# Where the late row blocks of W are staged, and in which order the transfers behind them are issued

## What is computed

```python
xc     = einsum('bct,bcd->bdt', x, w_cond[idx])             # 32 batches of 128 x 2048
result = einsum('bnd,od->bno', xc, W_base) + b_base          # 2048 x 2048 weights
logits = einsum('bnd,ed->bne', xc, W_gate)                   # 8 experts
route  = softmax(logits), top 2, renormalised
h      = einsum('bnd,erd->bner', xc, A)                      # rank 16
delta  = einsum('bner,eor->bno', h * route, B)
out    = x + result + delta
```

## Time and profile before

| | us |
|---|---|
| median of 3 runs | 1579.82 (1578.82 to 1580.52) |
| the profiled execution's own time | 1577.55 |
| its span, first to last instruction | 1575.7 |
| TensorE busy in the span | 1507.3 (96%) |
| VectorE busy | 1350.8 (86%) |
| ScalarE, GpSimd busy | 619.0 (39%), 645.7 (41%) |

### The profile page before, as it was taken

The page is one execution under the profiler, slowest core; times in us unless marked ns, Lnnn a source line. Parts: engine busy times, 40 slices in busy tenths (PEclk is TensorE's granted clock), DMA queues, the critical chain, the costliest instruction groups (busy, mean ns, idle before and its releaser), DMA issues.

```text
span 1575.7 us, 25846 instructions
## 1 busy us (share of the span) xinstructions
PE 1507.3 (96%) x9427; PEld 809.4 (51%) x9427; DVE 1350.8 (86%) x2258; ACT 619.0 (39%) x1016; POOL 645.7 (41%) x516
## 2 busy tenths in 40 slices
PE   5779999999999999999989999999999999999998
PEld 4554554555445554555545455555455555455553
DVE  6897999999899999999868888888888788888875
ACT  6665444444543445444413332223332223332321
POOL 3664555665666555665532122122122122122122
PEclk9899999999999999999999999999999999999999
DMA  5345555655555555655797343344343344333342
GB/s 192 108 158 166 163 163 166 191 169 167 152 165 171 166 160 178 179 185 155 220 344 246 105 127 101 95 141 130 113 124 93 105 141 124 118 116 93 114 111 74
DMA packets 169567, 235.95 MB, mean 150 GB/s; under 512 B 71898, under 2 KB 88794, under 8 KB 167130
## 3 DMA queue, kind: packets, MB, share of 16 engines
q1 hardware_dynamic: 167426, 219.63, 46.2%
q10 hardware_dynamic: 2016, 14.68, 2.4%
HBM read 147.83 MB, written 86.43 MB: 149 GB/s over the span
## 4 chain that ended last, share of the span: by engine, by line
PE 72%; DVE 15%; issue 5%; DMA 3%; POOL 2%; ACT 2%; SPq 0%; DVEq 0%; ACTq 0%; POOLq 0%
PE bank_x L1450 8%; PE bank_x L1451 8%; PE bank_x L1452 8%; PE bank_y L1452 8%; PE bank_y L1451 8%; PE bank_y L1450 8%; PE bank_z L1451 2%; PE bank_z L1452 2%; PE bank_z L1450 2%; DVE t_sums L1086 2%; PE bank_h L1452 2%; PE bank_h L1450 2%; PE bank_h L1451 2%; PE bank_c L1450 2%; PE bank_c L1452 2%
## 5 line engine op out<-in xcount | busy, mean ns | idle before, releaser
L608 POOL TENSOR_TENSOR x_res<-x_res,t_sums 128x512 f32<-128x512 f32 x255 | 350.2, 1376 | 847.6 <-DVE t_sums L1091 688.9
L1450 PE MATMUL bank_x<-TT,s_parts 128*128 128x512 f16 x768 | 294.4, 383 | 7.2 <-DVE s_parts L1061 5.9
L1451 PE MATMUL bank_x<-TT,s_parts 128*128 128x512 f16 x768 | 293.8, 383 | 0.0
L1452 PE MATMUL bank_x<-TT,s_parts 128*128 128x512 f16 x768 | 293.4, 382 | 0.0
L1450 PE MATMUL bank_y<-TT,s_parts 128*128 128x512 f16 x768 | 291.1, 379 | 2.3 <-DVE TT L1201 2.3
L1451 PE MATMUL bank_y<-TT,s_parts 128*128 128x512 f16 x768 | 291.1, 379 | 0.0
L1452 PE MATMUL bank_y<-TT,s_parts 128*128 128x512 f16 x768 | 291.1, 379 | 0.0
L716 ACT ACTIVATE p_copies<-bank_x,y_inv 128x512 f32<-128x512 f32 x128 | 87.7, 685 | 416.1 <-PE bank_x L1452 317.0
L1091 DVE TENSOR_TENSOR t_sums<-t_sums,inv_w 128x512 f32<-128x512 f32 x255 | 232.3, 911 | 8.7
L1061 DVE TENSOR_TENSOR s_parts<-a_full,s_parts 128x512 f16<-128x512 f32 x224 | 191.2, 870 | 33.7 <-ACT s_parts L701 33.7
L580 POOL TENSOR_TENSOR x_res<-x_res,BT 128x512 f32<-128x512 f32 x128 | 206.7, 1615 | 24.1 <-DMA x_res<-in_x_dram 22.8
(11 more groups left out here) (242 smaller groups left out, 2751.7 us busy)
## 6 DMA issues: line engine op xcount, KB each, us to landing
x<-in_x_dram SPq DMA_DIRECT2D x32, 1024.0 KB, 6.0
x_res<-in_x_dram SPq DMA_DIRECT2D x128, 256.0 KB, 4.0
part_scratch<-x_res SPq DMA_DIRECT2D x128, 256.0 KB, 3.0
x_res<-part_scratch SPq DMA_DIRECT2D x128, 256.0 KB, 4.0
out_dram<-x_res SPq DMA_DIRECT2D x128, 256.0 KB, 3.1
wt_scratch<-late_words SPq DMA_DIRECT2D x64, 224.0 KB, 3.5
TT<-wt_scratch ACTq DMA_DIRECT2D x14, 1024.0 KB, 9.2
x_parts<-in_L_ffn_W_base_dram SPq DMA_DIRECT2D x18, 512.0 KB, 6.6
```

The source lines that it names most:

```text
L608: nc.gpsimd.tensor_tensor(XR[:, xr_slot(m), :], XR[:, xr_slot(m), :], TM[:, m % 2, :], ALU.add).then_inc(r_added, 1)
L1450: nc.tensor.matmul(dst, lhs[0], rhs[0], start=start, stop=False, skip_group_check=chained)
L1451: nc.tensor.matmul(dst, lhs[0], rhs[1], start=False, stop=False, skip_group_check=chained)
L1452: return nc.tensor.matmul(dst, lhs[1], rhs[0], start=False, stop=stop, skip_group_check=chained)
```

## The change

Unit 5 is staged in the bias's place, unit 6 in x's place and unit 7 in A's place. The bias and step 1's x are loaded behind them. SyncE's order, ScalarE's, VectorE's, GpSimd's and TensorE's are rewritten to match; `w_scales` and the arithmetic are as before.

```diff
         def rows_of(g, i):
             if g < NU // 2:
                 return early_rows[(2 * g + i) % 4]
-            return (X, af_rows, xp_rows, af_rows)[g - NU // 2][:, i, :]
+            if g == NU // 2 + 1:
+                return bias[:, i * KH:(i + 1) * KH]
+            return (X, None, X, af_rows)[g - NU // 2][:, i, :]
...
@@ SyncE
             sp.wait_ge(w_tr, 4 * (NU // 2))
-            sp.dma_start(bias, b_base...).then_inc(bias_in, 16)
+            load_rows(5)
             for m in range(2, 4):
                 load_tile(m)
             sp.wait_ge(s_lo, NPROD)
-            load_rows(5)
-            sp.wait_ge(f_lo, 2)
-            sp.dma_start(ft_dram, FT_second...).then_inc(ft_out, 16)
+            load_rows(7)
             sp.wait_ge(b_lo, 1)
             sp.dma_start(bt_dram, BT_first).then_inc(bt_out, 16)
             sp.wait_ge(w_tr, 4 * 5)
+            load_rows(6)
+            sp.wait_ge(f_lo, 2)
+            sp.dma_start(ft_dram, FT_second...).then_inc(ft_out, 16)
+            sp.wait_ge(w_tr, 4 * 6)
+            sp.dma_start(bias, b_base...).then_inc(bias_in, 16)
+            sp.wait_ge(w_tr, 4 * 7)
             load_x(1)
-            sp.wait_ge(ft_out, 16)
-            load_rows(6)
             store_tile(0)
-            sp.wait_ge(w_tr, 4 * 6)
-            load_rows(7)
@@ GpSimd
+            w_lower(4)
+            w_lower(5)
             pool.wait_ge(bias_in, 16)
             add_bias(0)
+            add_r(0)
             add_bias(1)
-            w_lower(4)
-            add_r(0)
+            add_r(1)
+            w_lower(6)
             add_bias(2)
-            w_lower(5)
-            add_r(1)
             add_bias(3)
-            w_lower(6)
             add_r(2)
             add_r(3)
             w_lower(7)
@@ ScalarE
             nc.scalar.copy(inv_b[:, :], BD[:, 0:ER]).then_inc(agb_inv, 1)
+            sum_rows(5)
             copy_p(0, 0, P1_COPY)
             w_upper_first(4)
             copy_p(0, 0, P5_COPY)
-            sum_rows(5)
-            w_upper_rest(4)
+            upper(4, 2, B22)
+            upper(4, 3, B21)
+            sum_rows(6)
+            w_upper_sums(4, (T1, T3, T2, T4))
             copy_p(0, 0, U2_COPY)
             copy_p(0, 0, P4_COPY)
             w_upper_first(5)
-            sum_rows(6)
+            sum_rows(7)
             w_upper_rest(5)
-            sum_rows(7)
             w_upper(6)
             w_upper(7)
+            act.wait_ge(ft_out, 16)
             split_x_hi(1, 0)
@@ VectorE
             finish(0, 0, C11)
             w_first_sum(5)
-            find_maxima(1)
             w_scales(6)
             w_other_sums(5)
             finish(0, 0, C12)
             w_first_sum(6)
             w_scales(7)
             w_other_sums(6)
-            find_top(1)
             finish(0, 0, C21)
             finish(0, 0, C22)
             w_first_sum(7)
+            find_maxima(1)
+            w_other_sums(7)
+            find_top(1)
             scale_x(1)
-            w_other_sums(7)
             split_x_lo(1, 0)
@@ TensorE
             w_quad(6, 2)
             w_quad(6, 3)
+            w_quads(7)
             transpose_maxima(1)
-            w_quads(7)
             spread_maxima(1)
             pe.wait_ge(f_lo, 1)
```

More of the change, by code:

```diff
@@ L223, in adaln_ffn_kernel @@
         wc_in = sem("wc_in")
-        stage_in = [sem(f"stage{i}_in") for i in range(8)]
+        stage_in = [sem(f"stage{i}_in") for i in range(10)]
         a_in = sem("a_in")
@@ L394, in load_rows @@
                     o = s * KH + i * Q + r * P
-                    at = (2 * g + i) % 4 + 4 * (g // (NU // 2))
+                    at = 8 + i if g == NU - 1 else (2 * g + i) % 4 + 4 * (g // (NU // 2))
                     sp.dma_start(rows_of(g, i), w_base[o:o + P, k * KH:(k + 1) * KH]).then_inc(stage_in[at], 16)
@@ L459, in _ @@
             sp.wait_ge(w_tr, 4 * (NU // 2))
-            sp.dma_start(bias, b_base.rearrange("(a o) -> a o", a=1).to_broadcast([P, O])).then_inc(bias_in, 16)
+            load_rows(5)
             for m in range(2, 4):
@@ L463, in _ @@
             sp.wait_ge(s_lo, NPROD)
-            load_rows(5)
-            sp.wait_ge(f_lo, 2)
-            sp.dma_start(ft_dram, FT_second.rearrange("p f s n -> p (f s n)")).then_inc(ft_out, 16)
+            load_rows(7)
             sp.wait_ge(b_lo, 1)
@@ L469, in _ @@
             sp.wait_ge(w_tr, 4 * 5)
+            load_rows(6)
+            sp.wait_ge(f_lo, 2)
+            sp.dma_start(ft_dram, FT_second.rearrange("p f s n -> p (f s n)")).then_inc(ft_out, 16)
+            sp.wait_ge(w_tr, 4 * 6)
+            sp.dma_start(bias, b_base.rearrange("(a o) -> a o", a=1).to_broadcast([P, O])).then_inc(bias_in, 16)
+            sp.wait_ge(w_tr, 4 * 7)
             load_x(1)
-            sp.wait_ge(ft_out, 16)
-            load_rows(6)
             store_tile(0)
-            sp.wait_ge(w_tr, 4 * 6)
-            load_rows(7)
             for m in range(1, 4):
@@ L721, in sum_rows @@
                 for i in range(2):
-                    at = (2 * g + i) % 4 + 4 * (g // (NU // 2))
-                    act.wait_ge(stage_in[at], 16 * (g % (NU // 2) // 2 + 1))
+                    at = 8 + i if g == NU - 1 else (2 * g + i) % 4 + 4 * (g // (NU // 2))
+                    act.wait_ge(stage_in[at], 16 if g == NU - 1 else 16 * (g % (NU // 2) // 2 + 1))
                     junk_at = ((B22, B11) if g >= NU // 2 else (B11, T1))[i]
```

## The result

The changed kernel takes 1588.51 us (median of 4, 1587.07 to 1588.96) against 1579.67 beside it: a ratio of 1.0054, 95% interval 1.0037 to 1.0072, so slower, by 8.5 us (5.8 to 11.4 by the interval). The forecast was 1587.9. Its profiled execution took 1587.07 us with a span of 1585.3, 9.6 more than before.

A forecast was written before the change was run, and what follows sets the result against it. VectorE's list of work from 89.19 bounds W's preparation, and TensorE's first cond of step 1 sets the end. TensorE's order 5.7 plus clock 2.4 give 8.1 us; with the median 2.3 us above the execution, 1587.9 us, range 1582.5 to 1593.

The forecast's parts named there:

- The load of unit 6 and ScalarE's wait: SyncE issues unit 6's loads at about 79.6 and 80.0, landing at 87.3; ScalarE stands at sum_rows(6) from 77.1 until then.
- Start of VectorE's list: w_first_sum(5) on VectorE starts at 93.0 instead of 89.19, 3.8 us late, behind ScalarE's delayed copies.
- VectorE's list: VectorE's work from w_first_sum(5) to the end of w_other_sums(7): 24.93 us instead of 28.93, ending at 117.9.
- VectorE blocked more: Rival: three multiplies and unit 7's scales may each wait out a 1.27 us GpSimd operation; 3.4 us more, 1591.3; chance 0.12.
- The clause that the prediction quoted, on two SBUF inputs: Skill rule: a VectorE instruction with two SBUF inputs and a GpSimd one reading SBUF exclude each other for the whole instruction.
- The order on TensorE: TensorE stands at spread_maxima(1) from about 107.5 until 118.9; step 1's first cond comes at 127.0 against 121.26, 5.7 us later.
- The clock: After 11 us of TensorE idleness the granted clock drops; the features and first product lose about 2.4 us.
- The upper bound: Upper bound of the clock's loss: it grows 0.4 us for each us of TensorE idleness, 4.6 us.
- The mark as the end: The start of step 1's first cond, 121.26 before, is the mark: what it moves by, the end moves by.
- my signs of being wrong: Unit 6's rows landing before 83; find_top before 114; or the 3.44 us wait at 140.51 shrinking as the mark moves.
- The total: Whole kernel: 5.7 + 2.4 = 8.1 us slower, 1587.9 us, 0.5%.

The follow-up runs named there:

- b_rows6_first: The changed kernel with SyncE issuing unit 6's two loads ahead of the wait for b_lo and the store of B; ratio 1.0047 to the kernel before.
- g_pool_holds: The changed kernel with GpSimd holding its first bias add until VectorE has the scales of unit 7; ratio 1.0045 to the kernel before.
- the filler: The changed kernel with 38 unread matmuls of 128x512, 22 ahead of transpose_maxima(1) and 16 ahead of spread_maxima(1); ratio 1.0048 to the kernel before.
- a_maxima_late: The changed kernel with TensorE doing make_features(0) and product(0, 1, 0) ahead of transpose_maxima(1) and spread_maxima(1); ratio 1.0043 to the kernel before.
- the repeat: The changed kernel run and traced once more with nothing edited; ratio 1.0062 to the kernel before.

## Why the prediction was right, step by step

- *The load of unit 6 and ScalarE's wait*: right, by two errors that cancel. The second block's sum began at 87.02; the forecast had 87.3. But SyncE issued the pair at 78.38, not 79.6 (0.8 us earlier from the anchor: the store of B went out no later than before, 8.1 us from the anchor both times), and the second block took 8.6 us from there, not 7.7. b_rows6_first shows that what stands behind it moves with it.
- *Start of VectorE's list*: 92.67 against 93.0. From the anchor it is 3.9 us late, forecast 3.8.
- *VectorE's list*: mis-sized. From `w_first_sum(5)` to the end of `w_other_sums(7)` it took about 27.6 us, not 24.9. `w_scales(7)` alone took 5.1 us against 1.5 before, while `w_scales(6)`, with one long instruction beside GpSimd before (2.4 us), took 1.4; `find_top(1)` up to its diagonal took 1.8 us instead of 0.8. The forecast had put GpSimd's new order at nothing. This is the rival "VectorE blocked more" (3.4 us, chance 0.12) on top of the forecast: g_pool_holds brought `find_top` 3.3 us earlier. The Trainium skill (SBUF — State Buffer, Who interferes with whom) says that `tensor_scalar` can enter the two-port modes, in which VectorE and GpSimd exclude each other for a whole instruction. What was seen fits that: the instructions of `w_scales(7)` that grew are all TENSOR_SCALAR, and each ended with a GpSimd addition. The clause that the prediction quoted, on two SBUF inputs, is not the one that bears on these. That they ran in such a mode, and that it is a port and not something else of GpSimd's, no run here shows.
- *The order on TensorE*: right. It stood from 112.1 to 122.1 but for one transpose, 9.6 us of idleness in two pieces where the forecast had 11 in one, since the late scales had held unit 7's quadrants back as well. Putting two pieces of work ahead moved the first `cond` by 5.2 us, with the clock's loss still in it.
- *The clock*: 2.4 forecast, 2.2 measured, and taken away by the filler. The upper bound, a loss that grows with the idleness, is not borne out: 2.2 us behind 9.6 us of idleness here, 2.4 us behind 4.35 us in a_maxima_late.
- *The mark as the end*: only nearly. The first `cond` came 11.7 us late from the anchor, not 8.1: 2.7 + 1.0 us more on VectorE are nearly all of the difference. 0.8 us were given back at the next rows' wait (3.44 to 2.64 us, 2.63 in the repeat), since the rows' sum began 4.2 us after their issue instead of 5.0. I had taken this wait for no cushion, and its shrinking was one of my signs of being wrong; in the experiments it stretched from 2.6 to 9.3 us.
- *The total*: in part luck. The events give 10.9 us at the next scales, the forecast 8.1, and the runs 8.5 with an interval of 5.8 to 11.4, which holds both. The median of 1588.51 lies nearer to 1587.9 than the parts deserve. The forecast missed 3.7 us on VectorE and the 0.8 us given back at the rows' wait; that difference of some 3 us is less than the times of these few runs can tell.

## What to carry to other kernels

A buffer that is free early is no gain by itself: ask what its old tenant does to the transfers behind it, and on which engine's list the wait for the new one will stand. Here the load that was to be early stood behind a store that waits for VectorE, and the wait for it stood on ScalarE, ahead of the copies that VectorE needs. Putting the TensorE work ahead of the maxima was worth 5.2 us at the first `cond`: when a small result (four maxima) is put behind a long list on one engine, take the long work of the other engine ahead of the wait for it. And follow every moved operation through each queue: GpSimd's adds set SyncE's stores, and those set the loads of the next step.

## What was not expected of the hardware

38 matmuls whose results nobody reads, put into idle stretches of TensorE, brought the granted clock of the features' stretch from 0.50 to 1.00 and the first `cond` 2.3 us earlier. And beside four GpSimd adds of some 1.27 us a chain of seven small VectorE instructions took 5.1 us, against 1.4 with none beside it; with two adds and a lower part beside it, it took 4.05. Only its TENSOR_SCALAR instructions grew, each until the GpSimd operation beside it ended; the RECIPROCAL among them kept its 0.17 us. The size of the VectorE instruction did not protect it: the 4x4 scaling in `find_top(1)`, beside GpSimd's lower parts, took 1.17 us in the changed kernel against 0.22 before.
